# Two attention and two expert stages on one core: the instruction order of both attentions, the last batches' order and the clearing of expert regions changed

## The chip, the cores and the metric

One NeuronCore of one Trainium2 chip runs the whole program. The metric is the device time in microseconds (us) from the first to the last instruction, as the median of several executions.

## What is computed

The input x has 8 batches of 256 tokens with 128 features; a context of the same shape gives keys and values. Four steps follow, each added to x:

```
x += attn0(layernorm(x), ctx)   # 16 heads of 8, mask by equality of 0/1 flags, biases
x += moe0(layernorm(x))         # 8 experts, top 2, relu, hidden 512, weights by softmax of two logits
x += attn1(layernorm(x), ctx)   # 16 heads of 64, causal, output projection
x += moe1(layernorm(x))         # 8 experts, top 2, silu(x Wg) * (x Wu), hidden 352
```

## The kernel before

Each engine has its own instruction stream, written out by hand, and semaphores join them. The order of the work is the order of the Python calls in each engine's block; there is no planner. There are four stages.

**First attention** (`body0` and `last0` in each block). A batch has 8 slots of two heads (`R0 = 8`). In slot r of batch b, PE computes two sets of scores in one go (`scores0`, lines 440 and 446): those of batch b, transposed, whose exponentials ACT takes (L893), and those of the next batch c = b+1, of which DVE only takes the row maxima (L1166). The maxima are transposed (L457) and subtracted from the queries by `place_max` (L1173), in two halves, before batch c's own exponentials. Between the slots PE projects queries and keys (`project0`, L412, L413), multiplies the exponentials with the values (`mix0`, L474), turns the result back (`untranspose0`, L484) and does the routing of batch b-2: transpose (L492), logits (L501), prefix sums of the expert counts (L516 to L519). The maxima run a whole batch ahead, so there is an opening iteration b = -1 with maxima alone (8 slots) and a closing `last0` with exponentials alone (8 slots).

**Routing.** A batch leaves attention by `added0` and `stats` on DVE (L1191, L1115, L1119), the inverse root on POOL (L1592, L1594), the layer norm into `pay` (in the first attention on POOL, L1622; in the second on DVE, L1133), `choose` (the top two, L1199 to L1213) and `place` (each token's row in its expert's region, L1236, L1240) on DVE, and four indirect DMAs per batch from POOL (`send_one`, L1683). When the last batch is placed, DVE writes the ends of the regions (L1254) and a table of tiles; SP then clears the 128 rows behind each of the 8 ends, one DMA for each (L334, L335), waits for these, for the table and for all sends, and loads tiles of 128 rows (L345, L346).

**Experts** (`experts(l)`). 39 tiles; for each PE does a transpose (L655), the up-projection (L665), transposes (L676) and the down-projection (L686), and POOL scatters the rows into `results` (L1748), after DVE's copy (L1432 or L1435). The query, key and value weights of the second attention (`w1p`, three pieces of 512 KB) are loaded by POOL during the last batches (L1730, and the third at L1739), and split in a high and a low half by ACT (L1004) and DVE (L1440) ahead of the first expert stage.

**Second attention** (`prologue1`, `body1`, `epilogue1`). SP loads the results and the contexts of batches 0 and 1 (L352, L363), DVE combines (L1451) and normalises (L1133), POOL splits the context (`context_split`, L1583, L1585). PE then projects 4 units of queries, 4 of keys (L702) and 4 of values (L715). The body has 8 slots p for two heads each: scores (`scores1`, L729 to L735), maxima on DVE (L1467), exponentials on ACT (L1035), division on POOL (L1764, L1765), `turn1` (transposes, L748), DVE's copy (`pt_out`, L1489), `mix1` (L760, L763). In each slot PE does scores of slot p, a piece of the next batch's projections, `turn1` of slot p-2, `mix1` of slot p-3, another piece. Bank 7 of PSUM (`m`) is shared by projections, output, transposes, logits and prefix sums; each use waits for the one before it to be read.

The calls of one slot of `body1` on PE in the kernel before, cut short:

```
scores1(b, p, first)
if p == 0 and no(b) >= 2: prefix(1, d2, ...)
...                                   # a projection or value piece of batch c
if p == 7 and behind: transpose_t2(1, d, vv(c, 4) if ahead else None)
turn1(b, p - 2, first)
mix1(b, p - 3, first)
...                                   # a second piece
```

## Time and profile before

| | us |
|---|---|
| median of 3 executions | 800.55 (798.23 to 800.6) |
| the profiled execution, its own time | 807.82 |
| its span, first to last instruction | 806.0 |
| PE busy | 643.0 (80%) |
| DVE, ACT, POOL busy | 477.8, 391.9, 374.1 |

PE is the TensorE, DVE the VectorE, ACT the ScalarE, POOL the GpSimd, SP the engine that issues most DMAs. The kernel is a chain of stages with different limits, so the busy share of the whole says little; read the stretches one by one. The profiled execution is 7.27 us longer than the median.

### The profile page before, as it was taken

Reading aid. Unit: us, or ns where it says so; the run is one execution under the profiler, and the core shown is the slowest. Engines: PE = TensorE matmul, PEld = TensorE weight load, DVE = VectorE, ACT = ScalarE, POOL = GpSimd, SP = SyncE. Lnnn points to the kernel's source line nnn. Section 1 sums busy time; section 2 is a strip of 40 time slices with the busy share of each in tenths; the row PEclk is TensorE's granted clock in tenths of the full one; section 3 lists DMA queues with packets and bytes.
Section 4 is the critical chain, followed back from the end, with each engine's and each line's share of the span. In section 5 each row is a group of like instructions: output and inputs, shape, how many; then the busy total and the mean of one; then the engine's idle time right before and its main releaser. Section 6 shows DMA issues by size and latency. Waiting matters only on the chain.

```text
span 806.0 us, 16747 instructions
## 1 busy us (share of the span) xinstructions
PE 643.0 (80%) x5142; PEld 493.2 (61%) x5142; DVE 477.8 (59%) x1262; ACT 391.9 (49%) x1051; POOL 374.1 (46%) x579
## 2 busy tenths in 40 slices
PE   2778888888319999568999999898999884499990
PEld 1555555545207888456676767676766653399980
DVE  6767888764154555337657475757665663366664
ACT  2146766645115666346656564656565540133320
POOL 6062466545533555423434655554545563155551
PEclk9998999978558999879999999999999987699995
DMA  9010011100131212231000000001010100212115
GB/s 294 0 46 20 22 34 35 33 14 22 30 109 45 57 53 61 66 118 37 20 2 21 14 21 14 21 18 34 21 31 20 33 10 18 60 54 60 56 45 156
DMA packets 38522, 36.85 MB, mean 46 GB/s; under 512 B 5742, under 2 KB 34676, under 8 KB 38166
## 3 DMA queue, kind: packets, MB, share of 16 engines
q1 hardware_dynamic: 28230, 19.10, 8.3%
q0 software_dynamic: 5616, 12.11, 4.7%
q10 hardware_dynamic: 4592, 4.59, 2.0%
q8 instruction: 45, 0.74, 0.4%
q14 instruction: 39, 0.32, 0.1%
HBM read 25.11 MB, written 11.58 MB: 46 GB/s over the span
## 4 chain that ended last, share of the span: by engine, by line
PE 44%; DVE 15%; issue 15%; POOL 14%; ACT 5%; DMA 4%; SPq 2%; another core or an unknown queue 0%; POOLq 0%; DVEq 0%; ACTq 0%
PE ps L665 8%; PE ps L686 7%; POOL work L1765 5%; POOL dispatch L1683 4%; DVE work L1166 4%; PE ps L412 4%; PE ps L676 3%; PE ps L440 3%; PE ps L474 3%; DVE mx L1467 2%; POOL work L1764 2%; ACT work L1035 2%; PE ps L702 2%; PE ps L748 2%; DVE ra L1158 2%
## 5 line engine op out<-in xcount | busy, mean ns | idle before, releaser
L1035 ACT ACTIVATE work<-ps,nb 128x128 f32<-128x128 f32 (+1 forms) x256 | 104.1, 419 | 42.3 <-DVE nb L1474 37.7
L1748 POOL DMA_INDIRECT results<-work,dsti x78 | 76.3, 979 | 90.6 <-DVE work L1432 29.3
L1764 POOL TENSOR_TENSOR work<-work,rc 128x256 f32<-128x256 f32 x64 | 39.3, 613 | 152.7 <-DVE rc L1482 152.6
L1166 DVE TENSOR_REDUCE work<-ps 128x4 f32<-128x1024 f32 x64 | 78.4, 1225 | 32.2 <-PE ps L446 27.9
L665 PE MATMUL ps<-w_up,chib 128*128 x351 | 87.5, 377 | 2.0 <-issue 0.5
L1683 POOL DMA_INDIRECT dispatch<-pay,sloti x64 | 65.8, 1028 | 40.9 <-DVE sloti L1240 27.8
L1467 DVE TENSOR_REDUCE mx<-ps 128x6 f32<-128x768 f32 x64 | 61.0, 954 | 39.1 <-PE ps L735 38.6
L893 ACT ACTIVATE work<-ps 128x1024 f32<-128x1024 f32 x64 | 65.5, 1024 | 30.1 <-PE ps L440 28.2
L686 PE MATMUL ps<-w_dn,work 128*128 x546 | 74.3, 276 | 1.9 <-DVE work L1435 0.9
L702 PE MATMUL ps<-hl,ra 128*128 128x256 f32 x384 | 63.3, 306 | 7.5 <-ACT work L1011 4.4
L686 PEld LDWEIGHTS ps<-w_dn,work 128*128 128x128 f32 x546 | 67.1, 192 | 2.8 <-issue 2.7
L1489 DVE COPY work<-ps 128x768 f32<-128x768 f32 x64 | 60.9, 952 | 12.9 <-PE ps L748 12.4
L1765 POOL TENSOR_TENSOR work<-work,rc 128x512 f32<-128x512 f32 x64 | 66.4, 1038 | 0.0
L702 PEld LDWEIGHTS ps<-hl,ra 128*128 128x128 f32 x384 | 51.4, 198 | 23.6 <-ACT work L1011 13.2
L1011 ACT ACTIVATE work<-ps 128x512 f32<-128x512 f32 x64 | 38.6, 604 | 53.5 <-PE ps L702 53.0
L665 PEld LDWEIGHTS ps<-w_up,chib 128*128 128x128 f32 x351 | 58.2, 197 | 8.2 <-issue 6.0
L748 PE MATMUL ps<-cf,work 128*128 128x128 f32 x384 | 54.3, 279 | 6.2 <-POOL work L1765 6.0
L440 PE MATMUL ps<-ra 32*128 32x256 f32 x256 | 35.9, 357 | 24.0 <-DVE work L1166 12.7
L1035 ACT ACTIVATION_READ_ACCUMULATOR work<-ps,nb 128x1 f32 x256 | 51.9, 203 | 0.0
L748 PEld LDWEIGHTS ps<-cf,work 128*128 128x128 f32 x384 | 44.7, 143 | 11.7 <-POOL work L1765 8.6
L440 PEld LDWEIGHTS ps<-ra 32*128 32x128 f32 x256 | 22.7, 208 | 42.4 <-issue 31.3
L655 PE MATMUL ps<-cf,work 128*128 128x128 f32 x78 | 22.8, 292 | 31.0 <-DMA work<-dispatch 29.0
(164 smaller groups left out, 1409.7 us busy)
## 6 DMA issues: line engine op xcount, KB each, us to landing
work<-dispatch SPq DMA_DIRECT2D x78, 64.5 KB
stage<-in_wgu ACTq DMA_DIRECT2D x16, 176.0 KB
ct<-in_ctxT SPq DMA_DIRECT2D x16, 128.0 KB
w_dn<-in_w SPq DMA_DIRECT2D x1, 2048.0 KB, 9.5
stage<-in_w POOLq DMA_DIRECT2D x8, 256.0 KB, 3.2
ybuf<-results SPq DMA_DIRECT2D x16, 128.0 KB, 2.5
work<-results SPq DMA_DIRECT2D x8, 256.0 KB, 4.6
stage<-in_w1p POOLq DMA_DIRECT2D x3, 512.0 KB, 4.5
```

The lines of the kernel that those rows point to most:

```text
L440: mk = pe.matmul(ps[:, 2 + e, t * S:(t + 1) * S], kb[rows, par(b), g, t * P:(t + 1) * P], qb[rows, par(b), g, :], start=True, stop=True)
L665: mm = pe.matmul(ps[:, bank, 0:ff], ex[:, u % 2, i, :], w, start=(n == 0), stop=(n == 2))
L686: mm = pe.matmul(ps[:, 7, 0:D], ht[:, u % 2, k * P:(k + 1) * P], w_dn[:, bass.ds(e[u] * (cc * D) + k * D, D)], start=(k == 0), stop=(k == ...
L702: mm = pe.matmul(ps[:, bank, k * S:(k + 1) * S], w1p[:, w, i, (mm_ + k) * P:(mm_ + k + 1) * P], hl[:, par(c), w, j, :], start=(n == 0), st ...
L748: tr = pe.transpose(ps[:, 4 + e, k * P:(k + 1) * P], p1[:, pp % 2, e, k * P:(k + 1) * P], ident)
L893: act.activation(pt0[:, h:h + 2, :], ps[:, 2:4, :], ACT.Exp, scale=SC0).then_inc(s["b_exp"], 1)
L1035: ac = act.activation(p1[:, pp % 2, e, cols], bk[:, cols], ACT.Exp, scale=SC1, bias=nb1[:, pp % 2, e, t:t + 1], accum_out=rs1[:, pp % 2, e ...
L1166: ve.tensor_reduce(mx0[:, g // 2, :, k:k + 33:32].rearrange("p t e -> p e t"), ps[:, 0:2, :].rearrange("p e (t n) -> p e t n", t=QT), AX, ...
L1467: ve.tensor_reduce(mx1[:, r, :, :], ps[:, 2 * r:2 * r + 2, 0:3 * P].rearrange("p h (c n) -> p h c n", c=3), AX, ALU.max).then_inc(s["s_max ...
L1683: po.indirect_dma_start(xs[l], bass.IndirectOffsetOnAxis(ap=sloti[:, par(b), t, ch:ch + 1], axis=0), pay[:, par(b), t, ch, :], None, bound ...
L1748: po.indirect_dma_start(yc[l], bass.IndirectOffsetOnAxis(ap=dsti[:, k:k + 1], axis=0), ye[:, k, :], None, bounds_check=TOPK * T - 1, oob_i ...
L1765: po.tensor_tensor(p1[:, r, :, P:3 * P], p1[:, r, :, P:3 * P], rc1[:, r, :, 1:2].broadcast_to([P, 2, 2 * P]), ALU.mult).then_inc(s["s_norm ...
```

## The change

It does the following.

- Row maxima lead the exponentials by `LEAD = 6` slots and not 8: in slot r of batch b they are those of `leader(b, r)`. The opening iteration has 6 slots (`slots(b)`), and the first two slots of `last0` still have maxima. Around this the calls in `body0` are put in another order on all engines: the mix of batch b starts in its own slot 4, and a batch is normalised and routed one batch iteration earlier.
- The context has three buffers, filled by a ring over both attentions; the contexts of the second attention's batches 0 and 1 are loaded before the first experts and split before them. The weights `w1p` are loaded by SP, the third piece at tile 4 of the experts and split at tile 8.
- In `last0` POOL takes the last batch's root ahead of half of the sends of the batch before; DVE does the layer norm of the last two batches (before: POOL).
- ACT clears four of the eight region ends (`clear_ends`), SP the other four, in both layers.
- Second attention: keys and values of the first batch are projected before its queries, so before x is ready; in each slot `mix1` comes before `turn1`; the transpose for the routing is in slot 6 and not 7; `choose` is in slot 7 and not in slot 0 of the batch after; logits and prefix sums are put in spare columns of the score banks 2 and 0 and no longer in bank 7; POOL's root for `norm_out` comes before and not after the division of slot 4.

The core of the diff:

```diff
+LEAD = 6
...
-        ct = sb("ct", [P, 2, S])
+        ct = sb("ct", [P, 3, S])
...
-        ye = work[:, 4096:4096 + 4 * D].rearrange("p (r n) -> p r n", r=4)
+        ye = work[:, 3072:3072 + 4 * D].rearrange("p (r n) -> p r n", r=4)
...
+        def leader(b, r):
+            return (b, r + LEAD) if r + LEAD < R0 else (off(b, 1), r + LEAD - R0)
+        def slots(b):
+            return range(R0 - LEAD if no(b) < 0 else 0, R0)
+        def lg_at(l):
+            return ps[:, 2, 3 * P:3 * P + QT * E] if l else ps[:, 7, 0:QT * E]
+        def pfx_at(l):
+            return ps[:, 0, 3 * P:3 * P + (QT + 1) * E] if l else ps[:, 7, S:S + (QT + 1) * E]
...
             def tiles(l):
                 sp.wait_ge(*after(l, "ends_ready", 1))
-                for e in range(E):
+                for e in range(E // 2):
...
+            def clear_ends(l):
+                act.wait_ge(*after(l, "ends_ready", 1))
+                for e in range(E // 2, E):
+                    row = act.value_load(...)
+                    act.dma_start(xs[l][bass.ds(row, P), :], blank[:, :]).then_inc(s[f"slots_blank{l}"], 16)
...
@@ TensorE, body0
+                if here:
+                    scores0(b, 0)
+                    project0(c, 1)
+                    if behind2: logits(0, d2, None)
+                    values0(b, after(0, "qk_ready", 4 * no(c) + 1))
+                    scores0(b, 1)
+                    if behind: mix0(d, 3)
+                    if behind2: prefix(0, d2, after(0, "idx_done", 2 * no(d2) + 2))
+                scores0(b, 2)
                 project0(c, 2)
...
+                scores0(b, 3)
+                if behind: untranspose0(d)
+                project0(c, 3)
+                scores0(b, 4)
+                if here: mix0(b, 0)
+                if has2: transpose_x(0, c2, free)
+                scores0(b, 5)
+                if here: mix0(b, 1)
+                scores0(b, 6)
+                if has2: project0(c2, 0)
...
+                transpose_max(c, 0)
+                scores0(b, 7)
+                if here: mix0(b, 2)
+                if behind: transpose_t2(0, d, (s["qm_ready"], 2 * no(c) + 1))
...
@@ TensorE, last0, its end
+                scores0(b, 7)
+                logits(0, d, None)
+                mix0(b, 3)
+                prefix(0, d, after(0, "idx_done", 2 * no(d) + 2))
                 untranspose0(b, 0)
...
@@ TensorE, prologue1
+                for u in range(4): project1(c, u, u)
+                for n in range(3): values1(c, n, None, 4 + n)
+                values1(c, 3, qk(c, 1), 0)
                 transpose_x(1, c, None)
+                for u in range(4, 8):
+                    pe.wait_ge(*(qk(c, u - 2) if u < 7 else vv(c, 1)))
+                    project1(c, u, u - 3)
...
@@ TensorE, body1
+                    if p == 7 and behind: logits(1, d, None)
+                    mix1(b, p - 3, first)
...
+                    if p == 6 and behind: transpose_t2(1, d, vv(c, 2) if ahead else None)
                     turn1(b, p - 2, first)
...
@@ VectorE, last0
+                row_max(*leader(b, 0))
+                choose(0, d2)
+                row_max(*leader(b, 1))
+                place(0, d2)
                 place_max(b, 1)
                 attend0(d, (0, 1)); added0(d); stats(0, d, 1)
+                norm_out(0, d)
                 choose(0, d)
+                place(0, d)
                 attend0(b, (0, 1)); added0(b); stats(0, b, 1)
-                place(0, d)
+                norm_out(0, b)
...
@@ GpSimd, last0
-                leave0(d)
-                place0(d)
-                for w in range(2): po.dma_start(stage[:, w, :], ...)
-                leave0(b)
+                inverse_root(0, d, 1)
+                pack(0, d)
+                count_seen(0, d)
+                send_one(0, d, 0, 0)
+                send_one(0, d, 0, 1)
+                inverse_root(0, b, 1)
+                send_one(0, d, 1, 0)
+                send_one(0, d, 1, 1)
+                pack(0, b)
                 place0(b)
...
             experts(0)
-            context_split(1, (0, 0))
...
+            context_split(1, (0, 0))
+            context_split(1, (0, 1))
             experts(0)
```

## Rows read from the trace of the kernel before

**Rows 1.** Stretches of the span: length, busy us (x count) of each engine, clock

```profile
core 0: us, PE busy (x) PEld busy (x) DVE busy (x) ACT busy (x) POOL busy (x), PEclk, DMA share, GB/s
...
21.70:43.90 22.20, 16.77 (x79) 12.27 (x79) 16.33 (x38) 3.55 (x7) 1.29 (x2) 1.00 0.02 5
...
102.80:121.80 19.00, 16.23 (x192) 11.07 (x193) 16.58 (x32) 13.09 (x18) 13.01 (x21) 1.00 0.11 37
...
187.00:206.70 19.70, 15.45 (x183) 8.43 (x183) 4.94 (x23) 10.42 (x13) 12.89 (x22) 0.93 0.08 25
206.70:242.40 35.70, 5.57 (x33) 4.50 (x33) 13.27 (x53) 4.53 (x7) 13.52 (x20) 0.50 0.25 76
242.40:335.60 93.20, 89.88 (x624) 79.22 (x624) 46.19 (x156) 58.25 (x156) 44.65 (x77) 0.96 0.19 53
335.60:359.00 23.40, 11.38 (x62) 10.18 (x62) 6.08 (x21) 7.53 (x13) 5.37 (x10) 0.71 0.35 113
...
473.60:512.40 38.80, 36.69 (x298) 26.96 (x297) 24.84 (x70) 23.03 (x83) 21.10 (x32) 1.00 0.06 18
```

**Rows 2.** Timeline, first attention: start us, us, engine, line, operation; projections early and late

```profile
22.41 0.99 PE L412 MATMUL ps<-hl,ra 128*128 128x256 f32 x3
...
113.22 0.60 PE L412 MATMUL ps<-hl,ra 128*128 128x256 f32 x3
```

**Rows 3.** Timeline, from the end of the last mix to the first expert tile

```profile
206.73 0.60 ACT L898 ACTIVATE work<-ps 128x512 f32<-128x512 f32 x1 [1.77 <-PE ps L474]
...
212.51 0.25 DVE L1119 BATCH_NORM_AGGREGATE mv<-bn 128x2 f32<-128x6 f32 x2
...
213.95 1.10 POOL L1683 DMA_INDIRECT dispatch<-pay,sloti  x1 [3.42 <-DVE sloti L1240]
...
218.87 1.18 POOL L1730 DMA_DIRECT2D stage<-in_w1p  x2
220.05 0.28 POOL L1592 TENSOR_SCALAR var<-mv 128x2 f32<-128x2 f32 x1
...
221.33 1.58 POOL L1622 TENSOR_SCALAR pay<-x_sb,mv,rstd 128x128 f32<-128x128 f32 x2 [0.19 <-POOL rstd L1594]
...
227.04 0.19 DVE L1240 TENSOR_REDUCE sloti<-hp 128x4 uint32<-128x32 f32 x1
...
228.37 8.49 SPq L335 DMA_DIRECT2D dispatch<-blank  x8
...
232.24 0.97 POOL L1683 DMA_INDIRECT dispatch<-pay,sloti  x1 [0.30 <-issue]
...
240.60 6.02 SPq L346 DMA_DIRECT2D work<-dispatch  x6
```

**Rows 4.** The chain that ended last: start us, us, what; clearing and scattering DMAs

```profile
236.52 3.33 DMA dispatch<-blank
...
336.33 2.13 DMA results<-work,dsti
```

**Rows 5.** Timeline, from the last expert tile to the second attention's first scores

```profile
335.21 0.29 DVE L1432 TENSOR_TENSOR work<-ps,work 128x128 f32<-128x128 f32 x1 [1.56 <-PE ps L686]
...
347.66 7.98 PE L702 MATMUL ps<-hl,ra 128*128 128x256 f32 x48 [1.00 <-DVE hl L1152]
...
355.48 2.91 PE L715 MATMUL ps<-ra,hl 128*128 128x512 f32 x12
```

**Rows 6.** Timeline, PE in the second attention, batch 3, slot 7; below it a row of the page

```profile
506.45 0.44 PE L492 MATMUL ps<-cf,pay 128*128 128x128 f32 x2 [1.63 <-ACT work L1016]
...
L1489 DVE COPY work<-ps 128x768 f32<-128x768 f32 x64 | 60.9, 952 | 12.9 <-PE ps L748 12.4
```

**Rows 7.** Timeline, from the second attention's end to the first tile of its experts

```profile
683.80 8.09 SPq L335 DMA_DIRECT2D dispatch<-blank  x8
...
687.93 0.98 POOL L1683 DMA_INDIRECT dispatch<-pay,sloti  x1 [0.30 <-issue]
...
693.87 6.41 SPq L346 DMA_DIRECT2D work<-dispatch  x6
```

More of the change, by code:

```diff
@@ L356, in all_out @@
                     sp.wait_ge(*after(l, f"es_out{k}", 16 * len(range(k, NTILE, 4))))
+            sp.wait_ge(s["v_psum"], B)
+            sp.wait_ge(s["ctx_split"], B)
+            for k in range(2):
+                context(1, (0, k))
             tiles(0)
@@ L916, in body0 @@
             def body0(b):
-                c, c2, d, d2 = off(b, 1), off(b, 2), off(b, -1), off(b, -2)
-                has2, here, behind, behind2 = ahead(b, 2), ahead(b, 0), ahead(b, -1), ahead(b, -2)
-                for r in range(R0):
+                c, c2, d = off(b, 1), off(b, 2), off(b, -1)
+                has2, here, behind = ahead(b, 2), ahead(b, 0), ahead(b, -1)
+                for r in slots(b):
                     if here:
@@ L1524, in body1 @@
                         enter1(off(b, 2))
-                    if p == 4 and more:
+                    if p == 5 and behind:
+                        norm_out(1, d)
+                    if p == 6 and more:
                         norm_in(1, off(b, 2))
+                    if p == 7 and behind:
+                        choose(1, d, (2, 3))
                     for q in pieces(b)[p:p + 1]:
```

466 lines of the change are left out of this document (235 added, 231 removed).

## The prediction

> **What bounds the kernel now.** I read the page's slices first (which stretches are full on PE and which are not), then the busy time of each engine by stretch, then the timeline at the seams, the chain, and the waits inside the second attention. Times are from the profiled execution, 807.82 us.
>
> The stages have different limits. A batch of the first attention takes 19.0 us with PE at 16.2 and DVE at 16.6 [rows 1]: neither is full, because PE's scores for the maxima and DVE's maxima share one pair of banks and take turns. The experts are full on PE (89.9 of 93.2), and so nearly is the second attention, with 36.7 of 38.8 us in batch 3, against 24.8 on DVE, 23.0 on ACT and 21.1 on POOL [rows 1]. What is empty are the seams: 35.7 us from the last mix of the first attention to the first tile, with 5.6 us of PE work and the clock at 0.50, and 23.4 us between the experts and the first scores of the second attention, with 11.4 us of PE work at 0.71 [rows 1]. The opening iteration takes 22.2 us for one batch's maxima alone. The change touches all these places and leaves the tiles alone. So the seams decide, and the bodies only where PE is found waiting.
>
> **Part by part.**
>
> Opening of the first attention. Eight slots with maxima only, 22.2 us [rows 1], become six: two slots of 2.8 us are gone, 5.5 us. But `project0(c, 1)` and `values0`, which stood in them, go to slot 0 of the next iteration, where PE is slow still: three L412 take 0.99 us there against 0.60 later [rows 2], and a unit is six of these. About 2.5 us come back. Term: -3 (from -5.5 to 0).
>
> The seven paired bodies. The same instructions in another order. Adding what each slot asks of PE and of DVE, I get a new heavy slot 0 on PE (scores, a projection, logits, values) and a slot 3 with both `untranspose0` and a projection; DVE has at most one large extra in any slot. A wait for `place_max` gets two slots of slack, as before. Nothing is bought here, and the uneven slots may cost some tenths a batch. No row shows the new order; the bounds are a body like that of batch 2 or 3 (0) and PE's 16.2 us no longer overlapping the worst of slot 0, at most 1.5 us a batch (+10). I take +2, since DVE and PE each have over 2 us free in a batch. POOL now blocks on `place0(d2)` first and has the split of the context, the root, the norm and the weight piece queued behind; it is busy 13.0 of 19.0 us [rows 1], the context is due in slot 6 and the norm in slot 7, so I cost it at nothing; without that cover a late norm would hold PE in slot 7 for what it is late.
>
> `last0`. 19.7 us before [rows 1]. Three of batch 6's four mixes are done earlier; two slots of maxima are added on a DVE that is busy for 4.9 of 19.7 us. Term: -2 (-5 to +1).
>
> The routing of the last batch. Before, the statistics of batch 7 are done at 212.76, but its root starts at 220.05: POOL stands in the four sends of batch 6 (213.95 to 218.87) and then issues two weight DMAs (1.18 us) [rows 3]. After, batch 6's routing is ready earlier (its logits stand before the last mix), only two of its sends stand ahead of the root, and the weight DMAs are SP's. If those two sends fit before 212.8, the root goes at once: -7.3. The layer norm goes from POOL (L1622, 1.58 us for the pair [rows 3]) to DVE, which waits for it anyway: -1, as I take less than the whole. What follows (transpose to slots, until 227.23) is unchanged.
>
> Clearing. After the slots are written (227.04), SP issues eight clears in 8.49 us, 1.1 us each, the last landing 3.33 us after its start at 236.52 [rows 3, 4]; tiles load at 240.60. With four on each of two queues the clears end 4.3 us earlier, and then the last send is what ends last: it starts at 232.24 and a scatter lands 2.13 us after its start [rows 3, 4], some 234.4, and with the load's own issue 234.9: -5.7. ACT's clears stand ahead of the exponential of the weights and of the split of `w1p`; DVE's `weigh` waits behind these, and both are done by the time the first tile lands, as 6 us are free.
>
> Here a rule speaks against the change. Trace: eight issues hold SP for 8.49 us and the last one's landing takes 3.33 us [rows 3, 4], so most of the time is issuing. The Trainium skill, DMA: Bandwidth & Descriptors, section Issuing engines are not separate DMA queues, says that issuing from several engines saves only the sequencer's time, "which is usually small relative to the DMA itself". The rows have it the other way round here; the sum with the page's view is a rival below.
>
> First routing seam together: -7.3 -1 -5.7 = -14 (-17 to -6).
>
> Experts of layer 0. The third weight piece is now split within them. ACT is busy for 58.3 and DVE for 46.2 of 93.2 us [rows 1]; each gets one instruction more. Term: +1 (0 to +2).
>
> Experts to second attention. After the last copy (335.21) PE has nothing until the queries' projection at 347.66, then 48 matmuls of L702 in 7.98 us and 12 of L715 in 2.91 [rows 5], and scores start at 359. The key half (3.99) and the values (2.91) need only the context, which is now split 100 us earlier; they fit in the empty 12 us. That is -6.9 from the path. PE no longer comes from idleness with its clock at 0.71, and POOL has no context to split beside the root: -1.1. Term: -8 (-10 to -5).
>
> Second attention. In batch 3, slot 7, PE waits 1.63 us before the routing's transpose [rows 6]: bank 7 has first to be read by ACT, which has exponentials ahead of it. It is so in batches 2 to 6, and less in batch 1. In the new order the transpose stands in slot 6 behind `mix1`, with bank 7 read a slot earlier, and logits and prefix sums have columns of their own. Six times 1.63 is 9.8. What may come in its place: the prefix sums of slot 0 wait for DVE's `choose` in slot 7, which is behind a copy of 0.95 us [rows 6]; I take some 0.3 us a batch, 2 us, and give back 1 for the last batch, which also waits. `mix1` now follows the copy with only a second projection piece and the next scores between, which is twice that copy. Term: -9 (-13 to 0).
>
> Second routing seam. SP's clears start at 683.80 and take 8.09 us; the last send starts at 687.93 and would land 2.13 us later, at 690.1; tiles load at 693.87 [rows 4, 7]. With the load's issue -3 (-4 to -2).
>
> Sum: -3 +2 -2 -14 +1 -8 -9 -3 = -36. Against the execution's own 807.82 that is 771.8; the median of the runs is 7.27 less, and by it 800.55 - 36 = 764.5.
>
> **Rivals.**
>
> A. The first attention gets longer. For: its slots were even, and slot 0 is now heavy on PE; and its clock moves (0.93 in `last0`, 1.00 in batch 2 [rows 1]). At +1.5 us in each of seven bodies and nothing gained at either end: +10 in place of -3, so 777.5. Against: both engines have room. Chance 0.15.
>
> B. The second attention keeps its time: a wait in slot 0 or 7 takes the place of that in slot 7. For: DVE's `choose` now stands ahead of the maxima of slot 7, and `place` ahead of those of slot 0. Against: ACT, DVE and POOL are at 60% there [rows 1], so late maxima have two slots to catch up. -27 in all: 773.5. Chance 0.12.
>
> C. Two queues clear no faster than one, because the transfers themselves are what takes the time. Then only the 7.3 + 1 of the first seam stay, and nothing of the second: -36 + 5.7 + 3 = -27.3, so 773.2. The Trainium skill's sentence above would have it so. Against: 8.49 us of issue for eight [rows 3]. Chance 0.04.
>
> D. The early root is not early: batch 6's two sends are themselves late, and the root waits behind them. Half of 7.3 is lost: 768. Chance 0.07; it lies in the range anyway.
>
> E. Slower. Place: `mix1` right behind the scores in every slot of the second attention, with `turn1` after it. If DVE reaches its copy only when the next scores are done, PE waits for the whole copy, 0.95 us [rows 6], in each of some 56 slots: +53 in place of -9. The other parts stay at -27: 826.6. It decides from the point at which DVE comes to the copy more than about 1 us late, the time of the work between `turn1` and the next `mix1` less the copy. For: DVE has maxima, a reciprocal and the copy in one order. Against: DVE is idle for 14 of 38.8 us. Chance 0.04.
>
> That the change does not do what it says can be only for single parts, and is in B to D.
>
> **The numbers.** Forecast 0.58, A 0.15, B 0.12, C 0.04, D 0.07, E 0.04. The range for 8 in 10 takes in A to C and the terms' bounds, which seldom all fall on one side: 750 to 780. Some 0.3% (2.4 us) is what a measurement here tells from no change. Faster: all but E and a heap of A, B and C together, 0.94; the same 0.02; slower 0.04.
>
> **What would show it.** In the profile after: the root of batch 7 directly behind its statistics; the first tile load within 9 us of the last slots, with a send and no clear before it; four clears each on SP and ACT; key and value projections from right after the last expert copy, and scores some 3 us after the last query projection starts; no wait of over 1 us before L492's successor in the second attention, and a batch of 37.5 us instead of 38.8; the first attention's batch at 19.0 to 19.5. Wrong would be: PE waiting for DVE's copy in each slot, batches of 20 us and more in the first attention, or clears of 2 us each on ACT.

## The result, and the profile after

The changed kernel takes 755.48 us in the median of four runs (754.41 to 760.92), the kernel before 800.58 (798.23 to 801.95) beside it: a ratio of 0.9453, 95% interval 0.9403 to 0.9504, or 45.1 us. Run again beside two later experiments (e12 below), it took 755.98 in six runs (0.9448, 0.9394 to 0.9502). Forecast were 764.5 us and a range of 750 to 780. So the sign and the range held, and the gain came out 9 us larger than the 36 of the sum. The profiled execution after is at the median (755.54), the one before was 7.3 us above its own; the difference of the two profiles, 52.3 us, is therefore too large by that much. The first attention of one and the same program takes up to 8 us more or less in different profiles, with the place where PE's clock rises and falls, and the experiments have to be read with that in mind.

Both profiles are cut below at the same events: the first row maxima, the evacuation of the first attention's last mix, the last slots, the first tile load, the last result copied, the first scores, the first tile load of layer 1, the last result there. Length of each stretch in us, with three experiments that the next section describes (e8 is the kernel before with another clearing, e12 the changed kernel again); the last column is what the prediction gave the stretch.

| Stretch | before | e8 | changed | e12 | changed less before | forecast |
|---|---|---|---|---|---|---|
| first maxima to last mix | 185.0 | 180.4 | 162.3 | 162.6 | -22.8 | -3 |
| last mix to slots | 20.3 | 19.0 | 9.9 | 9.9 | -10.4 | -8.3 |
| slots to first tile load | 13.6 | 9.6 | 9.7 | 10.1 | -3.9 | -5.7 |
| experts of layer 0 | 94.6 | 96.0 | 94.4 | 94.8 | -0.2 | +1 |
| last copy to first scores | 23.9 | 23.6 | 18.1 | 17.9 | -5.8 | -8 |
| first scores to tile load of layer 1 | 334.8 | 337.9 | 320.6 | 320.0 | -14.2 | -12 |
| experts of layer 1 | 93.1 | 93.8 | 98.3 | 97.2 | +5.2 | 0 |

Each stretch but two comes near its forecast. The two are the first attention, 15 to 20 us better, and the experts of layer 1, 5 us worse, in a stage that the change does not touch. The experiments had to explain these, and to show that the others were right for the right reason.

The stretches of the profile after, same columns as [rows 1]: the opening iteration, a body of the first attention, its last batch, the seam, the experts, the way to the scores, a batch of the second attention.

```profile
21.63:38.00 16.37, 11.74 (x57) 8.54 (x58) 13.34 (x36) 2.52 (x5) 2.26 (x4) 1.00 0.00 1
99.00:117.50 18.50, 15.88 (x193) 10.82 (x191) 16.76 (x33) 13.19 (x18) 12.94 (x20) 1.00 0.12 37
168.68:183.88 15.20, 13.04 (x156) 7.83 (x156) 7.77 (x30) 10.47 (x13) 6.30 (x12) 1.00 0.23 71
183.90:205.30 21.40, 3.20 (x25) 2.38 (x23) 12.00 (x46) 3.07 (x5) 14.27 (x18) 0.63 0.18 53
205.30:298.20 92.90, 89.42 (x624) 78.21 (x624) 47.58 (x157) 58.88 (x157) 44.87 (x77) 0.97 0.21 59
298.20:315.95 17.75, 11.75 (x62) 10.47 (x63) 5.46 (x21) 7.55 (x13) 3.08 (x6) 0.81 0.50 163
426.15:464.28 38.13, 36.88 (x295) 27.10 (x295) 24.69 (x69) 23.21 (x83) 21.06 (x31) 1.00 0.06 19
```

The tiles have not moved (89.4 us of PE in 92.9). The opening lost 5.8 us and a batch of the second attention 0.7, in which PE is busy for the same time as before. The seam lost 14.3. The clock of 1.00 in the first row says little: the profile has no clock record before 41 to 79 us, by the run, and reads 1.00 there, but a weight load of the scores (L482) takes 306 ns in the median up to 45 us and 182 after 55 us, where it is 306 again when the clock is recorded at its lower level (e2, 168 to 178 us). So PE is at the lower level up to then, and its weight loads tell when it rises: at 50 us in the changed kernel.

The timeline of the seam after, which answers to [rows 3]:

```profile
183.88 0.60 ACT L942 ACTIVATE work<-ps 128x512 f32<-128x512 f32 x1 [1.19 <-PE ps L510]
...
185.32 1.09 POOL L1752 DMA_INDIRECT dispatch<-pay,sloti  x1 [1.24 <-DVE sloti L1304]
...
187.49 0.25 DVE L1181 BATCH_NORM_AGGREGATE mv<-bn 128x2 f32<-128x6 f32 x2
187.84 0.23 POOL L1661 TENSOR_SCALAR var<-mv 128x2 f32<-128x2 f32 x1
...
188.99 0.61 DVE L1195 TENSOR_SCALAR pay<-x_sb,mv,rstd 128x128 f32<-128x128 f32 x2 [1.24 <-POOL rstd L1663]
...
193.81 0.19 DVE L1304 TENSOR_REDUCE sloti<-hp 128x4 uint32<-128x32 f32 x1
...
195.07 3.58 ACTq L952 DMA_DIRECT2D dispatch<-blank  x4
...
195.13 3.74 SPq L365 DMA_DIRECT2D dispatch<-blank  x4
...
199.02 0.97 POOL L1752 DMA_INDIRECT dispatch<-pay,sloti  x1 [0.30 <-issue]
...
203.48 4.14 SPq L379 DMA_DIRECT2D work<-dispatch  x4
```

The first send of batch 6 comes 1.4 us after the last mix, where it was 7.2, because that batch's logits and slots are computed ahead of the mix. The root follows the statistics at once (187.84 after 187.74), the norm on DVE takes 0.61 us in place of POOL's 1.58, and four clears on each queue are issued in 3.6 and 3.7 us. The statistics themselves are done 3.9 us after the last mix and not 6.0: before, batch 6's transposes and logits stood between the mix and the last transposes on PE, and the clock was at its lower level (in e8, with a clock of 0.96 there, it was 4.7). But tiles load 9.7 us after the slots and not the 7.9 forecast. SP's waits in this stretch say why, last column the longest in us:

```profile
SPq L369 <- DMA dispatch<-pay,sloti: 3.7, 1, 3.7
```

The last send starts at 199.02. The chain of work that ended last shows its landing, and that of the second seam:

```profile
199.02 3.66 DMA dispatch<-pay,sloti
...
632.62 3.12 DMA dispatch<-pay,sloti
```

So it lands after 3.66 us, at 202.68, where the sum took 2.13 from a scatter of the experts' stage [rows 4]; in the second seam it is 3.12. SP then needs 0.8 us more until it issues the load at 203.48, where the sum took 0.5. The "4.4 us from start to landing" that e8's expectation below works with is these two together.

### The profile page after: what moved, and what is told of

The parts are those of the page before. It is cut to its first block, busy times and chain, and to the rows that moved or that the text cites. A ratio compares the mean times of both kernels' runs of the same rounds, so it can differ in the third digit from the quotient of the medians.

```text
span 753.7 us, 16723 instructions
## 1 busy us (share of the span) xinstructions
PE 622.7 (83%) x5142; PEld 481.3 (64%) x5142; DVE 480.9 (64%) x1266; ACT 393.8 (52%) x1051; POOL 371.2 (49%) x572
## 4 chain that ended last, share of the span: by engine, by line
PE 69%; DVE 15%; issue 6%; DMA 5%; POOL 3%; ACT 2%; SPq 1%; POOLq 0%; DVEq 0%; ACTq 0%
PE ps L704 9%; PE ps L741 7%; PE ps L725 7%; PE ps L788 5%; PE ps L800 5%; PE ps L448 4%; PE ps L813 4%; DVE work L1228 4%; PE ps L715 3%; PE ps L755 3%; PE ps L775 3%; PE ps L476 3%; PE ps L773 3%; PE ps L803 2%; PE ps L769 2%
## 5 line engine op out<-in xcount | busy, mean ns | idle before, releaser
L1087 ACT ACTIVATE work<-ps,nb 128x128 f32<-128x128 f32 (+1 forms) x256 | 104.3, 420 | 19.5 <-DVE nb L1540 12.6
L1228 DVE TENSOR_REDUCE work<-ps 128x4 f32<-128x1024 f32 x64 | 78.3, 1223 | 16.9 <-PE ps L482 15.2
L1087 ACT ACTIVATION_READ_ACCUMULATOR work<-ps,nb 128x1 f32 x256 | 51.9, 203 | 0.0
L476 PE MATMUL ps<-ra 32*128 32x256 f32 x256 | 33.3, 333 | 22.2 <-DVE ra L1220 15.9
L800 PE MATMUL ps<-work 128*64 128x256 f32 x256 | 41.8, 405 | 6.8 <-DVE work L1555 6.8
L1030 ACT ACTIVATE chib<-ps 128x128 fp32r<-128x128 f32 x78 | 21.7, 278 | 48.1 <-PE ps L694 45.3
```

The source lines that it names most:

```text
L800: pe.matmul(ps[64 * e:64 * e + 64, 6, c0:c0 + S], v1[:, par(b), 0, (2 * pp + e) * DK1:(2 * pp + e + 1) * DK1], pt1[:, pp % 2, e, 0:S], sta ...
L1087: ac = act.activation(p1[:, pp % 2, e, cols], bk[:, cols], ACT.Exp, scale=SC1, bias=nb1[:, pp % 2, e, t:t + 1], accum_out=rs1[:, pp % 2, e ...
L1228: ve.tensor_reduce(mx0[:, g // 2, :, k:k + 33:32].rearrange("p t e -> p e t"), ps[:, 0:2, :].rearrange("p e (t n) -> p e t n", t=QT), AX, ...
```

## The experiments

A difference given with a plus or minus is one to the changed kernel's 755.48 us, or, between stages, to its profile; a ratio is to the kernel before, run beside it. The experiments ran on three chips, and the kernel before took 802.2 to 803.9 us beside them (812.6 beside e11) in place of 800.58; by the ratios the differences in medians come out some 2 to 5 us smaller than printed for e1 to e5. Single medians are therefore weak for the small parts, and the stretches of the profiles carry them.

**e1: the clears back on one queue.**

```diff
-                for e in range(E // 2):
+                for e in range(E):
...
-            clear_ends(0)
...
-                clear_ends(1)
```

> The changed kernel with all eight clears back on SP in both routing seams, nothing else touched. Theory: issuing is what takes the time, about 1.05 us a clear, so eight on SP end at 195.13 + 8.5 = 203.6 in the first seam and at 628.51 + 8.1 = 636.6 in the second, and land 2 to 3 us later; the first tile loads then start about 3 us later than now in the first seam (206.5 against 203.48) and 2 us later in the second (638.6 against 636.52). In all +5 us, 760 to 761. Rival (C of the prediction): the transfers take the time whoever issues them; then the loads start where they do now and the kernel stays at 755.5. Second rival: the sends end both seams now and would hide some of the clears; then less than 3 us.

Measured 758.56 us (757.69 to 764.12), +3.1; its ratio of 0.9465 (0.9412 to 0.9518) is not distinct from 0.9453. In the profile the slots are 12.0 us ahead of the tile load (9.7 with two queues) and 11.2 in the second seam (9.1): +2.4 and +2.1. SP's waits ahead of the tiles, of this kernel:

```profile
SPq L378 <- DMA dispatch<-blank: 1.4, 1, 1.4
```

So with one queue the clears end last, with two the sends. The rival that the transfers take the time whoever issues them falls, by these rows and by e8; the gain is what lies between two ends, and so less than the 5.7 + 3 of the sum.

**e2: all four sends of batch 6 ahead of the root of batch 7.**

```diff
-                inverse_root(0, b, 1)
                 send_one(0, d, 1, 0)
                 send_one(0, d, 1, 1)
+                inverse_root(0, b, 1)
```

> The changed kernel with all four sends of batch 6 ahead of the root of batch 7 on POOL, where now two stand ahead of it and two behind. Theory: the statistics of batch 7 are ready when the second send ends, so each further send ahead of the root costs its 1.4 us: root at 190.7 in place of 187.84 and first tile load 2.9 us later, 758.4. Rival: the end of this seam is set by something that this moves not at all (clears, tables), so 755.5.

Measured 763.8 us (760.2 to 766.62), +8.3. From the last mix to the slots it takes 12.5 us in place of 9.9, +2.5 (theory 2.9), and to the tile load another 1.0 more. The rest of the 8 us lies ahead of the place that was edited: the first attention took 170.4 us in this profile and 162.3 in that of the changed kernel, with the same instructions. The stretches 140 to 200 us of e2, and under them of the changed kernel, columns as in [rows 1]:

```profile
140.00:160.00 20.00, 17.10 (x206) 11.63 (x205) 18.14 (x35) 14.45 (x20) 12.58 (x20) 1.00 0.19 57
160.00:180.00 20.00, 16.93 (x155) 10.05 (x155) 13.73 (x28) 10.36 (x13) 8.70 (x15) 0.66 0.17 52
180.00:200.00 20.00, 12.43 (x111) 7.23 (x111) 6.12 (x29) 6.59 (x8) 10.41 (x17) 0.76 0.08 28
```

```profile
140.00:160.00 20.00, 17.37 (x205) 12.14 (x203) 18.19 (x36) 13.59 (x18) 12.57 (x20) 1.00 0.19 57
160.00:180.00 20.00, 15.57 (x202) 9.07 (x205) 13.81 (x32) 13.70 (x17) 11.60 (x19) 1.00 0.20 62
180.00:200.00 20.00, 6.48 (x65) 4.12 (x57) 11.07 (x55) 4.37 (x8) 11.05 (x19) 0.74 0.17 50
```

Up to 160 us they are alike. Then the granted clock of e2 is at 0.66 over 20 us, which is its lower level (1.2 GHz) for most of them, and PE does 155 matmuls in 16.9 us in place of 202 in 15.6. With this, and with first bodies that are 1.7 us longer, 8 us are gone. It is the same effect that stood in the profile of the kernel before without my having priced it.

**e3: keys and values behind the queries' input.**

```diff
                 c = (0, 0)
+                transpose_x(1, c, None)
                 for u in range(4):
                     project1(c, u, u)
...
                 values1(c, 3, qk(c, 1), 0)
-                transpose_x(1, c, None)
```

(and `x_high` on ACT likewise)

> The changed kernel with the transpose of the queries' input ahead of the key and value projections in the prologue of the second attention, on PE and ACT; the context is split as early as now. Theory: keys and values (3.1 and about 3.5 us of PE) then wait with the queries for the combined result and the layer norm, and lie on the path again: from the last expert copy to the first scores 24 to 25 us in place of 18.1, the kernel +6 to +7, 761.5 to 762.5. Rival: the idle stretch of 4 us on PE, after which the queries' projections run at the half clock, is gone or moved, so that the projections together run faster and only some 4 us come back, 759.5.

Measured 763.27 us (762.46 to 767.41), +7.8 (by the ratio, 0.9522, some 5.5). From the last copy to the scores it takes 22.6 us in place of 18.1, +4.5: the rival's number. PE in this stretch of the changed kernel, then of e3:

```profile
298.42 3.10 PE L741 MATMUL ps<-hl,ra 128*128 128x256 f32 x24 [0.71 <-DVE work L1497]
...
301.36 2.91 PE L755 MATMUL ps<-ra,hl 128*128 128x512 f32 x12
...
309.71 2.69 PE L741 MATMUL ps<-hl,ra 128*128 128x256 f32 x11 [1.09 <-DVE hl L1214]
...
311.77 3.40 PE L741 MATMUL ps<-hl,ra 128*128 128x256 f32 x15
```

```profile
313.96 2.92 PE L755 MATMUL ps<-ra,hl 128*128 128x512 f32 x12
...
316.72 3.03 PE L741 MATMUL ps<-hl,ra 128*128 128x256 f32 x24
...
320.53 0.38 PE L769 MATMUL ps<-cbi 128*128 128x256 bf16 x2 [0.78 <-ACT work L1063]
```

In the changed kernel keys and values lie in the gap at full clock, as forecast. PE then has next to nothing from 304 to 309.7 us, and the 24 matmuls of the queries take 5.5 us at the half clock; in e3, where they stand behind other work, 3.03. The move saves the 6.9 us and gives 2.4 back. The other 3 to 5 us of e3's median are not the prologue's: in its profile the second attention is 5.0 us longer, with a granted clock of 0.72 and 0.60 from 610 to 630 us, in code that is the same.

**e4: the second attention in the old order** (bodies and epilogue on PE, ACT, DVE and POOL as before, routing sums in bank 7).

```diff
                 def body1(b, ahead, behind):
...
-                    if p >= 3:
-                        mix1(b, p - 3, first)
...
                     if p >= 2:
                         turn1(b, p - 2, first)
...
+                    if p >= 3:
+                        mix1(b, p - 3, first)
...
-            return ps[:, 2, 3 * P:3 * P + QT * E] if l else ps[:, 7, 0:QT * E]
+            return ps[:, 7, 0:QT * E]
```

> The changed kernel with the whole body and epilogue of the second attention (PE, ACT, DVE, POOL) in the order of the kernel before, routing sums back in bank 7; prologue, first attention and both seams as now. Theory: the 12.4 us that the second attention (first scores to last output projection) lost are the order's own; it takes 312 to 313 us again in place of 300.4, the kernel +12.4, 768. Rival: a steady batch gains only 0.65 us in the trace, and what came besides (in the last batches, where the weights of the experts are split) was chance or the clock's; then +4 to +6, 760 to 761.5.

Measured 769.55 us (767.32 to 771.49), +14.1. By the profile the stretch from the scores to the tiles is 331.7 us in place of 320.6, +11.1. PE's waits in a steady batch of the changed kernel and, below, of e4 (us, times, longest):

```profile
PE ps L553 <- DVE hots L1275: 0.7, 1, 0.7
PE ps L741 <- DVE hl L1214: 0.4, 1, 0.4
```

```profile
PE ps L528 <- ACT work L1068: 1.6, 1, 1.6
PE ps L741 <- ACT work L1063: 0.2, 1, 0.2
```

The wait of 1.6 us is gone and 1.1 us of new ones have come, so that a steady batch gains 0.65 us and six of them 3.9. The rest of the 11 us stands in the last two batches and the epilogue: from the last `x_high` to the tiles it takes 94.4 us in the changed kernel and 102.4 in e4. In e4 the granted clock is 0.79 from 610 to 620 us there and stays at 1.00 in the changed kernel, so a part of the 8 us is the clock's. In e3, in the changed order, a clock that was lower still (0.72, then 0.60) cost 5.0 us over this whole stage; so more than 3 of the 8 us are the order's own, as an estimate from these two profiles.

**e11: transposes ahead of the mix, all else as changed.**

```diff
-                    if p >= 3:
-                        mix1(b, p - 3, first)
-                    elif behind:
-                        mix1(d, 5 + p, False)
                     if ahead:
...
                         turn1(d, 6 + p, False)
+                    if p >= 3:
+                        mix1(b, p - 3, first)
+                    elif behind:
+                        mix1(d, 5 + p, False)
```

> The changed kernel with the order of mix and transposes in a slot of the second attention as before (transposes of the probabilities of slot p-2, then the mix of slot p-3 behind them), the routing's transposes, logits and sums where the change put them. Theory: the wait of 1.63 us is gone because the routing's transposes moved and its sums have columns of their own, whichever of mix and transposes comes first; the mix first is worth nothing in the steady batches, where PE waited for no copy before, so a batch stays at 38.1 to 38.3 us and the kernel at 755 to 757. Rival: the mix first gives the routing its slack; with the transposes first some wait returns in slot 0 or 7, a batch takes 38.8 again and the kernel is at 760. Rival (E of the prediction, read the other way): the mix first costs PE waits now, and undoing it gains, 37.5 us a batch, 751.

Measured 804.32 us, 0.9894 (0.9825 to 0.9962) of the kernel before beside it (812.6), where the changed kernel is at 0.945: about 36 us lost. None of the three expectations was near. Its first attention, in the same code, took 182.8 us, with a clock of 0.90 to 0.93 from 80 to 180 us, and the kernel before was 9 to 12 us slower beside it than beside the others; the batches of the second attention are at full clock and can be compared. One takes 42.3 us in place of 38.1, and PE's waits in 45 us of it are

```profile
PE ps L741 <- ACT work L1062: 3.6, 3, 1.2
PE ps L741 <- DVE hl L1213: 1.4, 1, 1.4
PE ps L755 <- ACT xnt L945: 1.0, 1, 1.0
PE ps L553 <- DVE hots L1274: 0.7, 1, 0.7
```

Bank 7 is read by ACT and DVE between two uses, and PE stands until they have. But the order of transposes and mix alone does not make this: e4 and the kernel before have the transposes ahead of the mix in each slot too, and there a batch takes 38.8 us with 1.8 us of waits, as e4's rows above show. What e11 keeps and e4 does not is the order of the other engines. In the changed kernel ACT takes the mix's result (L1094 here) ahead of its copy from bank 7 (L1062); in the kernel before it took it behind the slot's first copy and the exponentials. From the timeline of e11:

```profile
441.77 0.60 ACT L1094 ACTIVATE work<-ps 128x512 f32<-128x512 f32 x1 [6.25 <-PE ps L803]
442.27 0.59 ACT L1062 ACTIVATE work<-ps 128x512 f32<-128x512 f32 x1
...
442.91 0.74 PE L741 MATMUL ps<-hl,ra 128*128 128x256 f32 x4 [1.18 <-ACT work L1062]
```

ACT stands 6.25 us for a mix that now comes late in PE's slot, the copy waits behind it, and PE waits for the copy. ACT waits 13.8 us in all for the mix in these 45 us, in four places. So PE's mix first and ACT's order belong together; the mix first in the old ACT order was not run.

**e5: three parts undone at once** (e1, e3 and e4 together).

> The changed kernel with three parts undone at once: all clears on SP, keys and values behind the queries' input, and the whole second attention in the old order. What stays of the change is the first attention (order, lead of six slots, three context buffers), the early root, and the weights and context that SP loads. Theory: the parts add up. From the three runs that undid them singly (+3.1, +7.8, +14.1 over 755.5) 780.5; the remaining 20 us below the kernel before are the first attention's and its seam's. Rival: the parts overlap, since a part undone gives another one cover; then 774 or less, or 786 or more. In the profile: slots of the last batch at 193 to 194 us if the clock holds through the first attention, at 203 to 205 if it falls in its last third, as it did in the run with the four sends first.

Measured 776.64 us (775.32 to 776.68), 0.9682 of the kernel before (0.9638 to 0.9725). The three parts cost 25.0 singly and 21.2 together by the medians. By the ratios, each to the kernel before beside it, they cost 2.1% singly and 2.3% together, so within the noise they add up, and the difference between chips is enough for the 4 us. What is left, 25.6 us, is in the main the first attention and its routing. In the profile: 162.3 us to the last mix (185.0 and 180.4 in the old order) and 9.9 to the slots (20.3 and 19.0), that is -18.1 and -9.1 against the better of the two old profiles. Both old profiles are of executions 5 to 7 us above their medians, so in the median the first attention gives less than in them: 25.6 less the routing's 9.1 to 10.4 leaves some 15 to 17 us, as an estimate (the other stretches of e5 differ from those of the kernel before by up to 3 us, some up and some down).

**e8: the kernel before with clears on two queues.**

```diff
-                for e in range(E):
+                for e in range(E // 2):
...
+            clear_ends(0)
             weight_exp(0)
```

(`clear_ends` as in the changed kernel, in the second seam too)

> The kernel before, with four of the eight clears of each seam on ACT's queue and nothing else. Theory: then the last send ends the first seam; started at 232.24 and 4.4 us from start to landing as in the changed kernel, it lets the tiles load at 236.8 in place of 240.6, -3.8; in the second seam 687.93 + 3.9 = 691.8 in place of 693.87, -2. In all -5.8, 795 against 800.5 to 803.9. Rival: the 5.7 + 3 of the prediction, 792 to 795. Rival: nothing. The profile also shows whether the two long last bodies of the first attention (21.8 and 23.8 us) and the 93.1 us of layer 1's experts come back in a second execution of the kernel before; theory: the long bodies are the clock's and need not, the experts' time does.

Measured 797.25 us against 802.22, 0.9943 (0.9914 to 0.9973): -5.0. Slots to tiles are 9.6 us and 8.9, from 13.6 and 11.2: -3.9 and -2.3, as the theory had it. It also gives the old order a second profile, from which the first attention can be read. The first maxima start at 21.55 us in e8 and at 21.63 in the changed kernel, the last (64 in each) at 176.32 and 171.40. From first to last maxima the new order saves 5.0 us, and 13 more lie behind the last maxima: 25.7 us to the last mix in e8 (176.32 to 201.97), 22.7 in the kernel before, 12.5 in the changed kernel. The last maxima do not stand at the same place, though: in the old order all of `last0` comes behind them, in the new one six of its eight slots. Cut as the prediction cut it, the changed kernel against e8 has -5.8 us in the opening, -4.7 in the seven bodies and -7.6 in `last0`. At full clock an old body takes 18.5 to 19.0 us and a new one 18.5.

`last0` from its first scores to the last mix, columns as in [rows 1]: e8 and e2. The changed kernel has 15.2 us at full clock (third row of the stretches above), the kernel before 19.7 at 0.93 [rows 1].

```profile
179.16:201.97 22.81, 19.59 (x184) 10.89 (x183) 4.91 (x23) 10.76 (x14) 12.97 (x22) 0.70 0.07 21
```

```profile
171.99:192.09 20.10, 18.75 (x157) 11.14 (x156) 7.95 (x30) 10.44 (x13) 6.24 (x12) 0.63 0.14 47
```

With the clock low in both (e8 and e2; e9 as e2) the new order takes 2.7 us less, and near full clock in both (the kernel before and the changed one) 4.5 less; it has 156 matmuls there and the old one 183. The other 5 us against e8 are the clock's.

The clock also holds part of the bodies' 4.7. PE in 10 us of the first bodies, changed kernel and under it e8:

```profile
60.00:70.00 10.00, 8.64 (x109) 5.82 (x111) 8.14 (x12) 7.19 (x11) 0.00 (x0) 1.00 0.05 13
```

```profile
60.00:70.00 10.00, 9.31 (x68) 6.75 (x67) 6.19 (x7) 5.50 (x7) 2.79 (x5) 1.00 0.05 15
```

By the weight loads the clock rises at 50 us in the changed kernel and at 71 in e8, and the first two bodies together are 2.7 us shorter. Whether the new order brings this rise forward, or it differs by the execution as the fall does, is not shown: it came at 41 to 56 us in the eleven profiles with six slots of lead (in four of them with a relapse), and at 60 (with a relapse) and 71 in the two old ones.

**e10: a lead of five slots.**

```diff
-LEAD = 6
+LEAD = 5
```

(with the third shared maxima of the last batch, and a projection's base moved one slot)

> The changed kernel with maxima that lead by five slots in place of six (opening iteration of five slots, three shared slots in the last batch); nothing else is moved, so that the transposes of the maxima stand right behind the last maxima that they need. Theory from the result: each slot of lead costs an opening slot (2.8 us) and in the last batch an unshared one, and six in place of eight gave 5.8 in the opening; five give 2.5 more there, but PE now waits for DVE's last maxima in slots 2 and 6 of each body, some 1.3 us twice a batch as far as DVE is not caught up later, so that a body takes 19 to 20.5 us in place of 18.5: +4 to +10, 759 to 765. Rival: PE's slack (16.5 of 18.5 us busy) swallows these waits, and the kernel gains 2 to 4 us, 752 to 753.

Measured 786.15 us in six runs (777.56 to 798.57), two of which lie over 795. The ratio of the other four is 0.9743 (0.9682 to 0.9805), about 24 us more than the changed kernel's 0.9448 beside it. From the third on the bodies take 19.5 to 19.8 us in place of 18.5, as expected; but the first sixteen maxima take 51.9 us in place of 41.8, which no theory had, and the first attention 186.6 us in all. In the first bodies PE is full, and at the lower clock by its weight loads (327 ns from 60 to 75 us):

```profile
60.00:70.00 10.00, 10.00 (x68) 6.66 (x71) 4.73 (x5) 4.83 (x6) 0.00 (x0) 1.00 0.05 15
...
80.00:90.00 10.00, 9.30 (x104) 5.95 (x104) 9.06 (x14) 7.07 (x9) 7.17 (x12) 1.00 0.09 28
```

Its clock rose only at 79 us, that of the changed kernel at 50; why so late is open. So six slots of lead are better than five in this order. Eight slots, or the old lead, in the new order of the calls were not run, so what the lead and what the order is worth is not separated.

**e6, e7, e9: the experts of layer 1.** Every profile with the changed kernel's SP and POOL showed them at 96 to 99 us. e6 gives eight buffers to the results on their way out, e7 puts layer 1's in the old columns, e9 is e6 with the copy of the targets moved.

```diff
-        dsti = sb("dsti", [P, 4], U32)
+        dsti = sb("dsti", [P, 8], U32)
...
-        ye = work[:, 3072:3072 + 4 * D].rearrange("p (r n) -> p r n", r=4)
+        ye = work[:, 3072:3072 + 8 * D].rearrange("p (r n) -> p r n", r=8)
```

(e6; with eight semaphores es_out)

```diff
-        ye = work[:, 3072:3072 + 4 * D].rearrange("p (r n) -> p r n", r=4)
+        ye = [work[:, c:c + 4 * D].rearrange("p (r n) -> p r n", r=4) for c in (3072, 4096)]
```

(e7)

```diff
                 for t in range(NTILE + 3):
+                    if t < NTILE:
+                        k, k8 = t % 4, t % 8
...
+                        po.tensor_copy(dsti[:, k8:k8 + 1], xt[:, k, D:PAY].bitcast(U32)).then_inc(s["e_dst"], 1)
                     u = t - 3
                     if u >= 0:
...
-                    if t < NTILE:
-                        k = t % 4
```

(e9)

> The changed kernel with eight buffers in place of four for the experts' results on their way out (ye, dsti and the semaphores of the scatters), nothing else. The experts of layer 1 take 96 to 99 us in all profiles of the changed kernel, 93.1 in that of the kernel before, with the same three pauses at tiles 27, 32 and 33. Theory: GpSimd copies the rows' targets of tile t only when the scatter of tile t-4, issued 3 us earlier, has landed; SP's next tile load waits for that copy; when two landings are late PE runs dry, 2.3 us, and comes back at the half clock. With eight buffers no scatter is waited for: the pauses go, layer 1's experts take 92 to 93 us, and the kernel 750 to 751. Rival: the pauses come from the tile loads themselves or from instructions being fetched; then 755.5 and the same pauses.

> The changed kernel with layer 1's results on their way out in the columns of the kernel before (4096 on, in place of 3072); layer 0 as now. Rival to the run before this: where the buffer lies decides (its neighbours are written by PE's helpers at the same time), and with it the 5 us come back, 750.5. Theory: the place costs nothing, 755.5 with the pauses at tiles 27, 32 and 33.

> The kernel with eight result buffers, and in GpSimd's loop over the tiles the copy of tile t's targets ahead of the scatter of tile t-3 instead of behind it. The run with eight buffers alone kept the pauses, so the wait for a landing is not their cause. Theory now: GpSimd makes some stops of 2 to 3 us at the same places in every profile of the changed kernel (2.94 us at 69 us into layer 1's experts, 1.9 at 66, 2.9 at 80) and the targets' copy stands behind them in its order, with the result of three tiles ago ahead of that; SP's load of tile t+3 waits for the copy, and so PE runs dry at tiles 27, 32 and 33. With the copy first the load depends on PE's transpose and on a copy that waits for nothing else; layer 1's experts then take 93 us in place of 98.3, layer 0's 94, and the kernel 750. Rival: the stops hit the copy as well wherever it stands, or the loads are late for another reason: 755 to 756 and the same pauses.

e6: 757.05 us, experts of layer 1 98.4, the same pauses; the theory that a landing was waited for fell. e7: 755.58, 98.8: the place is nothing. The timeline of the changed kernel at tile 32:

```profile
705.88 0.19 POOL L1826 COPY dsti<-work 128x1 uint32<-128x1 uint32 x1
...
709.01 0.98 POOL L1819 DMA_INDIRECT results<-work,dsti  x1 [2.94 <-DVE work L1502]
...
712.36 5.42 SPq L379 DMA_DIRECT2D work<-dispatch  x3
...
714.41 0.33 PE L694 MATMUL ps<-cf,work 128*128 128x128 f32 x1 [2.27 <-DMA work<-dispatch]
...
714.70 1.73 PE L704 MATMUL ps<-w_up,chib 128*128 x6
```

POOL stops for 2.94 us ahead of a scatter, the copies of targets behind it are late, SP's loads wait for these, PE waits 2.27 us and comes back with six matmuls in 1.73 us in place of 1.21. In e9 the same stop is there,

```profile
712.82 0.19 POOL L1821 COPY dsti<-work 128x1 uint32<-128x1 uint32 x1
...
715.95 0.98 POOL L1827 DMA_INDIRECT results<-work,dsti  x1 [2.94 <-DVE work L1504]
...
716.44 0.30 PE L696 MATMUL ps<-cf,work 128*128 128x128 f32 x1
```

but the copy is already done and PE does not notice: 93.9 us in place of 97.2 in e12 and of 98.4 in e6, from which it differs only by the copy's place. The releaser that the profile names for the stop, a copy of DVE, had been done in e9 since 713.07; what POOL stops for is open. The kernel as a whole took 756.14 us (750.14 to 760.56), e12 755.98.

**e12: the changed kernel again.**

> The changed kernel as it is, beside the two variants above on the same chip. Expected 755.5 (754 to 761), the pauses in layer 1's experts at the same three tiles, and the clock full through the first attention, or in one execution in four low from about 164 us on, with 5 to 8 us more.

Measured 755.98 us (753.48 to 764.45). Its times lie in two groups, 753.5 to 756.0 four times and 762.4 to 764.5 twice; those of e9 at 750.1 to 752.4 and 759.9 to 760.6, three times each. The profiled e9 is of the upper group, with the first attention at 170.3 us and the clock at 0.82 and 0.50 from 160 to 180 us; that of e12 is of the lower, with 162.6. So e9's median says nothing of the 3.3 us that its experts gained, and the lower groups, 3 to 4 us apart, do: it is the fastest kernel of this study by its stages, but its ratio of 0.9407 (0.9351 to 0.9463) is not distinct from 0.9448.

## Why the prediction was right or wrong, point by point

**Opening, -3: too small.** It lost 5.8 us, all of two slots. The 2.5 us that I put back for work moved to slot 0 did not come: from maximum to maximum the first body takes 20.7 us, the old ones 21.4 and 22.4 (e8).

**Seven bodies, +2: right** at full clock (18.5 against 18.5 to 19.0 us). Of the 12.4 us that the seven bodies are shorter in the profile after, 8.6 are those of the last two, where PE's clock was at 0.78 and 0.79 over 160 to 200 us in the profile before.

**`last0`, -2: within its bounds** (2.7 to 4.5 us less at a like clock, bounds -5 to +1); the 7.6 us against e8 have 5 of the clock in them.

**The first attention as a whole, -3: the step that failed.** It is -18 against e8, some 15 to 17 in the median (e5), more than the 9 us by which the sum fell short. The prediction reckoned all three terms as if PE's clock were the same on both sides. The runs show it otherwise: in the old order the clock rose later and fell before the last mix in both profiles; in the new order it held up to the last mix in seven of eleven profiles. That it held in the profiled execution is partly luck, since it fell in e2, e6, e9 and e11; what of it the order brings about stays open. I had the row that could have warned me, a clock of 0.93 in [rows 1], and used it only against the change, in rival A, for which nothing was found.

**First seam, -14: right in sum (-14.3), wrong in its parts.** The early root gave 7.2 of the forecast 7.3 and the norm 1.1 of 1. The other 2.1 of the 10.4 us lie ahead of both: the statistics come 3.9 us after the last mix and not 6.0, which the sum had not priced; by e8's 4.7 (an estimate from one profile) 0.8 of it is the order and 1.3 the clock. The clears gave 3.9 and not 5.7: the landing of the last send is 3.7 us and not 2.13, a price taken from another stage, and the load's issue 0.8 and not 0.5.

**Rival C, two queues clear no faster: wrong** (e1, e8). The Trainium skill, DMA: Bandwidth & Descriptors, section Issuing engines are not separate DMA queues, calls the sequencer's time usually small beside the DMA itself; here four issues take 3.7 us on one queue, eight 8.1 to 8.5, and sharing them gains 2.1 to 3.9 us a seam. The measurement decides.

**Experts to scores, -8: mechanism right, 2 us less** (-5.8; e3 has 4.5 for the move alone). The term missed that a gap of PE that is only moved keeps the queries at half clock.

**Second attention, -9: right in size, not in place, and so in part by luck.** The wait went as said, but what took its place is 1.1 us and not 0.3, as rival B had it. The six batches gave 4 us where 9.8 less 2 were forecast; the end of the stage, which the term had at 1, gave what they did not. Rival E's wait for DVE's copy did not come: no wait of PE in a steady batch is over 0.7 us. Turned round on PE alone, the order costs 31 us in this stage (e11), mostly because ACT in its new order then stands for the mix.

**Second seam, -3: -2.1** (-2.3 in e8), by a landing of 3.1 us and not 2.13. **Experts of layer 1, 0: +5**, not foreseen: a chain of POOL, SP and PE with no slack, set off by stops of POOL (e9).

## What to carry to other kernels

Where two engines share banks and one has to lead, count the slots in which either works alone at both ends of the loop: two fewer at the opening gave 5.8 us here. When one engine's order is changed, look at the orders of those that serve it: an engine that takes a late result first holds up the copy behind it (ACT in e11). A copy that lets the next load go should not stand in its queue behind a scatter that needs a result of three tiles ago.

## What the runs showed of the hardware that was not expected

The granted clock fell to its lower level at 164 to 167 us in some executions of one and the same code (e2, e6, e9) and only at 189 to 190 us, behind the last mix, in others (the changed kernel, e12, e1). From the last maxima to the last mix e2 and e9 took 16.1 us in place of 12.5, and their whole first attention is 8 us longer, of which the first bodies have some 1.7. PE's weight loads also became fast at different times, from 41 to 79 us, and until then the profile, which has no clock record there, reads 1.00. One profile of each of two kernels can differ by that much in a stage that both share, so a stage is to be compared in more than two profiles.

A scatter of the experts' results took 2.13 us from start to landing [rows 4]; a send of the routing took 2.4 in the median of the changed kernel's 64, and 3.66 and 3.12 as the fourth of four beside eight clears. They write to different tensors, and which of the two sets the time was not separated. And POOL stopped for 2.94 us at the same place of layer 1's experts, 68 to 70 us in, in the profile of the changed kernel and in those of e1 to e7 and e9 to e12; past the first tiles the two profiles of the old program have no stop of over 2 us there.
